# A state-space model and a feed-forward layer with looked-up weights: the order inside the layers' slots, and one gathered weight group fewer

## The chip, the cores and the metric

The kernel runs on one core of a Trainium2 chip. The core has five engines that run beside each other and meet in semaphores: TensorE (PE in the profile; its weight loads are PEld), VectorE (DVE), ScalarE (ACT), GpSimd (POOL) and SyncE (SP), which only starts transfers here. The metric is the time of one execution on the device, in microseconds (us): the median of three runs was 1264.0 us (1263.94 to 1266.96).

## The reference

The input x has 2048 tokens of 512 numbers. Two blocks follow each other, each added to its input and normalized over the 512 numbers:

```python
x = _layernorm(x + _L0_attn_ref(x, ...), axis=-1)
x = _layernorm(x + _L0_ffn_ref(x, codebook, idx_gate, idx_up, idx_down), axis=-1)
```

The first block projects to 64 numbers a token and runs four layers, then projects back to 512. A layer is

```python
y = silu(layernorm(h, l1w, l1b))
y = sconv(y, pr + 1j * pi, lr + 1j * li)      # a convolution along the tokens with p ** t, p complex
h = h + y * scl
y = layernorm(h, l2w, l2b)
y = silu(einsum('bld,fd->blf', y, w1) + b1_)  # 64 -> 256
h = h + einsum('blf,df->bld', y, w2) + b2_    # 256 -> 64
```

The second block has three weight matrices, which are not given but looked up: each index picks 8 numbers of a codebook of 8192 rows.

```python
Wg = codebook[idx_gate].reshape(1376, 512)    # also Wu, and Wd of 512 x 1376
h = silu(x @ Wg.T) * (x @ Wu.T)
return h @ Wd.T
```

## The kernel before, in words

**Weights.** The 1376 inner rows are cut into eleven tiles k of 128 (the last has 96, `REST`). Each tile has a gate unit 2k and an up unit 2k + 1. A unit has four turns of four quads; a quad is a quarter of a turn. PE looks a quad up: DVE compares the low index bits with constants and writes one-hots (`one_hots`, L1057), PE multiplies the codebook (in two parts) by them in eight matmuls (`candidates`), DVE keeps the candidate whose high bits fit (`choose`, L1075), and after the four quads of a turn PE adds up with four small matmuls against `adder` (`add_up`). The indices of a quad are spread over the partitions by a transfer of SP (`spread_parts`). At the end of a unit ACT copies the sum as the weight's high part (`keep_picked`, L459) and DVE makes the low part (`keep_rest`). For some units, listed in `POOLED`, the first turn isn't looked up: POOL gathers its 16 columns with 16 indirect transfers (`gather_up`, L389), and PE adds them with sixteen transposes (`turn_up`). `POOLED` holds the ten up units below 20 and the gate units of the tiles in `BOTH`. The down weights are all gathered by POOL (`gather_down`, L400, 16 x 4 for each full tile), and PE transposes them (`turn_down`, L924). `UP_AFTER` says after how many groups of 16 down gathers each `gather_up` stands in POOL's queue.

**The layers.** h is kept as 64 channels (twice, for the real and the imaginary part) by 2048 tokens, cut in `NC` = 4 chunks of 512. One slot t is one chunk c = t % 4 in one layer l = t // 4; there are 16. PE, DVE and ACT each have a written order for a slot, and the parts of several items lie in one slot: the first half of item t, the second norm and the 64-to-256 product of item t - 2, the way back of item t - 3. In each slot one or two quads of the look-up are placed as well (two in slots 0, 4, 8 and 12). The steps: `square1`, `variance1`, `root1`: the first norm; `xn`, Silu, `u`: its product and the turning back by `tab`; the scan (L1304) gives `g`; `d`, whose semaphore is `damped`, is g times `tab`; `turn` (L652, one column) carries the state to the next chunk, and DVE copies it (`state`, L1282). `mixed` is the matmul of d by `mix` into bank 0, `add_mixed` adds it to h. Then `square2`, `variance2` (into bank 2), `root2`, `norm2` (L1260), `spread` (two matmuls by w1t, into banks 1 and 2), `silus` (two Silus, which read these banks), `back` (two matmuls by w2t into bank 0) and `add_back` (L1267). Bank 2 thus serves `turn`, `variance2` and `spread`, and bank 0 serves `mixed` and `back`.

**Behind the layers** come the projection to 512, the norm, the transposes of x (`project`, `turn_x1`), then ten tiles k in each of which PE alternates a quad of a later tile's look-up with a share of tile k's gate and up products (`hidden`), and for each pair of tiles 16 products with the down weights (`down`). The last tile and its `down` end the kernel; their down weights are POOL's last gathers.

Matmuls recorded through the helper `mm` all have line L652, DVE's two-operand steps through `tt` line L1033.

Of the kernel before, what the change touches and what calls it, by code (L numbers as in the profile page):

```python
# [25 lines left out]
def build(nc, a, out):  # L26
# [6 lines left out]
    NC = T // C  # L33
# [15 lines left out]
    BOTH = (0, 5)  # L49
    POOLED = sorted([2 * k + 1 for k in range(FULL)] + [2 * k for k in BOTH])  # L50
    UP_AFTER = (0, 0, 4, 7, 13, 17, 20, 24, 25, 26, 30, 33)
# [16 lines left out]
    ITEMS = L * NC  # L68
# [91 lines left out]
    with ctx:  # L160
# [115 lines left out]
        s = {n: sem(n) for n in sem_names}  # L276
# [135 lines left out]
        def _(act):  # L412
# [130 lines left out]
            for t in range(ITEMS):  # L543
                root1(t)
                if t >= 2:
                    root2(t - 2)
                lay = cols[:, t // NC, :]
                act.wait_ge(s["normed1"], t + 1)
                if t:
                    act.wait_ge(s["scanned"], t)  # L550
                act.activation(y, xn, ACT.Silu, bias=lay[:, LN1_B:LN1_B + 1], scale=lay[:, LN1_W:LN1_W + 1]).then_inc(s["silu_made"], 1)
                if t:
                    square2(t - 1)
                if t >= 2:
                    silus(t - 2)
                square1(t + 1)

                act.preload_act_table(ACT.Abs_reciprocal_sqrt)
                while kept < unit_of(quads_in(t)[0]):
                    keep_picked(kept)  # L560
                    kept += 1


            root1(ITEMS)
# [85 lines left out]
        def _(pe):  # L650
# [197 lines left out]
            def mixed(i):  # L848
                pe.wait_ge(s["damped"], i + 1)
                if i >= 3:  # L850
                    pe.wait_ge(s["h_made"], i - 2)
                mm(bank[0][:, :], mix[:, i // NC, :], d).then_inc(s["mixed"], 1)
# [18 lines left out]
            def back(i):  # L871
                pe.wait_ge(s["ff_made"], i + 1)
                pe.wait_ge(s["h_mid"], min(ITEMS, i + 3))
                if i:
                    pe.wait_ge(s["h_made"], i)
                for k in range(FK):
                    done = mm(bank[0][:, :], w2t[:, i // NC, k, :], ff[:, k, :], k == 0, k == FK - 1)
                done.then_inc(s["ff_back"], 1)
# [10 lines left out]
            for t in range(ITEMS):  # L889
                quads = quads_in(t)  # L890
                if t % NC:

                    pe.wait_ge(s["scanned"], t)
                    if t >= 3:
                        pe.wait_ge(s["ff_made"], t - 2)
                    mm(bank[2][:, 0:1], turn[:, t // NC, :], g[:, C - 1:C]).then_inc(s["rotated"], 1)
                if t:
                    mixed(t - 1)
# [5 lines left out]
                candidates(quads[0])  # L904
                if t >= 2:
                    spread(t - 2)
                for quad in quads[1:]:
                    candidates(quad)
                for quad in quads:
                    add_up(quad - 1)  # L910
# [112 lines left out]
        def _(v):  # L1023
# [253 lines left out]
            for t in range(ITEMS):  # L1277
# [5 lines left out]
                if t:  # L1283
                    add_mixed(t - 1)
                one_hots(quads[0] + 1)
                v.wait_ge(s["rs1_made"], t + 1)
# [7 lines left out]
                if t >= 2:  # L1294
                    norm2(t - 2)
                if t >= 3:
                    add_back(t - 3)
                v.wait_ge(s["silu_made"], t + 1)
                tt(u, y, tab[:, l, :], ALU.mult).then_inc(s["turned_back"], 1)
                v.wait_ge(s["turned_back"], t + 1)  # L1300
                if c:
# [3 lines left out]
                                     ).then_inc(s["scanned"], 1)  # L1305
                v.wait_ge(s["scanned"], t + 1)
                if t:
                    v.wait_ge(s["mixed"], t)
                tt(d, g, tab[:, l, :], ALU.mult).then_inc(s["damped"], 1)
                choose(quads[0])  # L1310
                for quad in quads[1:]:
                    one_hots(quad + 1)
                    choose(quad)
# [125 lines left out]
```

## Time and profile before

| | us |
|---|---|
| median of three runs | 1264.0 |
| profiled execution | 1264.5 |
| its span, first to last instruction | 1262.5 |
| PE busy | 1188.8 (94%) |
| DVE busy | 1011.6 (80%) |
| POOL busy | 929.9 (74%) |
| ACT busy | 261.7 (21%) |
| mean granted clock of PE | 0.982 |

The busy time of an engine is the sum of its instructions, overlaps counted once. Idle time is put down to whoever released the engine. The page's chain follows the end of the program back; where two engines finish close to each other it names only the later one. The layers run from about 88 to 240 us, the tiles k = 0 to 9 from about 290 to 1200 us, and the rest is the last tile.

### The profile page before, as it was taken

To read this page: it belongs to the slowest core of one execution; us is meant where nothing else is said; L and a number is where in the kernel's file an instruction comes from. 1 tells how busy PE (TensorE), PEld (TensorE's weight loads), DVE (VectorE), ACT (ScalarE), POOL (GpSimd) and SP (SyncE) were. 2 spreads that over 40 slices of the span, in tenths; PEclk is the share of its full clock that TensorE was granted. 3 is DMA by queue.
4 is the path that set the end of the run, shared out by engine and by line. 5 is a ranking of instruction groups with operands and counts; after the bars stand their busy time and mean duration, and the time that the engine had idled before them with its cause. 6 is when DMAs were issued, how large, how long until landed. Compare 5 with 4: busy or idle time off the path is not lost.

```text
span 1262.5 us, 16835 instructions
## 1 busy us (share of the span) xinstructions
PE 1188.8 (94%) x5595; PEld 839.3 (66%) x5595; DVE 1011.6 (80%) x2194; ACT 261.7 (21%) x395; POOL 929.9 (74%) x895
## 2 busy tenths in 40 slices
PE   6857998889999999999999999999999999999998
PEld 4533444346777777777777777777777777778876
DVE  3998898878997778888777888778888778888845
ACT  2325777772000000000000000000000000000024
POOL 6777777777777777777777777777777777777710
PEclk8968999989999999999999999999999999999999
DMA  9331211102433223433223433333433333334303
GB/s 202 64 68 37 45 37 39 27 4 53 105 92 87 65 71 80 95 82 92 65 69 79 89 85 81 65 70 86 93 85 87 67 70 79 94 72 88 60 2 133
DMA packets 96971, 93.57 MB, mean 74 GB/s; under 512 B 53549, under 2 KB 57909, under 8 KB 96886
## 3 DMA queue, kind: packets, MB, share of 16 engines
q1 hardware_dynamic: 64692, 83.86, 23.0%
q0 software_dynamic: 28160, 3.66, 8.5%
q10 hardware_dynamic: 4034, 4.98, 1.4%
q8 instruction: 45, 0.74, 0.3%
q14 instruction: 40, 0.33, 0.1%
HBM read 87.53 MB, written 4.90 MB: 73 GB/s over the span
## 4 chain that ended last, share of the span: by engine, by line
POOL 73%; issue 21%; PE 4%; DMA 1%; DVE 0%; ACT 0%; POOLq 0%; SPq 0%; DVEq 0%
POOL stage_down L400 57%; POOL stage_up L389 16%; PE bank L652 2%; PE cand L652 2%; DMA work<-in_L_ffn_idx_up 0%; DMA stage_down<-in_L_ffn_codebook,idx_down 0%; ACT x L505 0%; POOLq L160 0%; DVE chosen L1229 0%; DVE x L1033 0%; PE bank L924 0%; SPq L315 0%; DVE idx_low L1091 0%; DVE idx_low L1092 0%; DVE shift L1239 0%
## 5 line engine op out<-in xcount | busy, mean ns | idle before, releaser
L400 POOL DMA_INDIRECT stage_down<-in_L_ffn_codebook,idx_down x688 | 722.3, 1050 | 209.7 <-issue 209.1
L652 PE MATMUL cand<-one_hot,book 128*128 128x512 f32 (+1 forms) x2432 | 622.7, 398 | 19.0 <-DVE one_hot L1057 19.0
L1057 DVE TENSOR_SCALAR one_hot<-bc,low_of 128x512 fp32r<-128x512 uint16 (+1 forms) x1216 | 512.8, 482 | 99.0 <-PE cand L652 97.3
L652 PEld LDWEIGHTS cand<-one_hot,book 128*128 128x128 f32 x2432 | 449.7, 189 | 187.2 <-DVE one_hot L1057 51.8
L389 POOL DMA_INDIRECT stage_up<-in_L_ffn_codebook,idx_up x192 | 205.6, 1071 | 63.8 <-issue 58.2
L652 PE MATMUL bank<-x1t_hi,w 128*128 128x512 f32 (+1 forms) x704 | 239.1, 396 | 0.0
L1075 DVE SCALAR_TENSOR_TENSOR chosen<-bc,high_of,cand 128x512 f32<-128x512 uint16 (+1 forms) x304 | 220.2, 724 | 21.1 <-PE bank L652 17.9
L652 PEld LDWEIGHTS bank<-x1t_hi,w 128*128 128x128 f32 (+1 forms) x704 | 130.3, 185 | 31.4 <-issue 2.1
L652 PE MATMUL bank<-x1t_lo,w 128*128 128x512 f32 (+1 forms) x352 | 137.7, 391 | 0.0
L598 ACT ACTIVATE prod<-bank 128x512 f32<-128x512 f32 (+1 forms) x44 | 26.3, 599 | 389.4 <-PE bank L652 389.4
L605 ACT ACTIVATE act_hi<-prod 128x512 fp32r<-128x512 f32 x40 | 25.3, 633 | 342.5 <-DVE prod L1033 342.5
L652 PE MATMUL bank<-wd,act_hi 128*128 128x512 f32 x272 | 84.5, 392 | 3.1 <-DVE x L1033 3.1
L652 PE MATMUL bank<-chosen,adder 128*32 128x512 f32 (+1 forms) x608 | 79.0, 591 | 0.0
L1033 DVE TENSOR_TENSOR x<-x,bank 128x512 f32<-128x512 f32 x76 | 51.7, 681 | 33.3 <-PE bank L652 33.3
L652 PEld LDWEIGHTS bank<-x1t_lo,w 128*128 128x128 f32 (+1 forms) x352 | 65.2, 185 | 15.8 <-issue 1.4
L652 PEld LDWEIGHTS bank<-wd,act_hi 128*128 128x128 f32 x272 | 50.8, 188 | 15.6 <-DVE x L1033 4.8
L652 PE MATMUL bank<-wd,act_lo 128*128 128x512 f32 x136 | 53.2, 391 | 0.0
L1033 DVE TENSOR_TENSOR prod<-prod,bank 128x512 f32<-128x512 f32 (+1 forms) x44 | 29.9, 679 | 22.1 <-PE bank L652 22.0
L459 ACT ACTIVATE w<-bank 128x512 fp32r<-128x512 f32 (+1 forms) x22 | 12.9, 588 | 118.4 <-PE bank L652 118.4
L652 PE MATMUL bank<-work,mean_p 64*128 64x512 f32 x72 | 28.1, 706 | 7.9 <-issue 7.1
L652 PE MATMUL bank<-work,w2t 128*128 128x512 f32 x64 | 34.4, 663 | 0.4 <-issue 0.4
L427 ACT ACTIVATE work<-bank,eps 128x512 f32<-128x512 f32 x36 | 23.2, 683 | 29.6 <-PE bank L652 29.5
(181 smaller groups left out, 751.8 us busy)
## 6 DMA issues: line engine op xcount, KB each, us to landing
bc<-index_parts SPq DMA_DIRECT2D x272, 256.0 KB, 3.3
stage_down<-in_L_ffn_codebook,idx_down POOLq DMA_INDIRECT x688, 2.7
bc<-index_parts_rest SPq DMA_DIRECT2D x32, 192.0 KB, 3.1
x<-in_L_attn_x ACTq DMA_DIRECT2D x4, 1024.0 KB, 9.8
out_x<-x SPq DMA_DIRECT2D x16, 256.0 KB, 2.0
stage_up<-in_L_ffn_codebook,idx_up POOLq DMA_INDIRECT x192
index_parts<-parts_t SPq DMA_DIRECT2D x20, 32.0 KB, 2.0
w_in<-in_L_attn_W ACTq DMA_DIRECT2D x2, 256.0 KB
```

The costliest lines, as they stand in the source:

```text
L389: pool.indirect_dma_start(stage_up[n % UPS][:, j * CS:(j + 1) * CS], None, a["L0_ffn_codebook"], bass.IndirectOffsetOnAxis(ap=idx_up[:, pl ...
L400: pool.indirect_dma_start(stage_down[k % RING][:, q, j * CS:(j + 1) * CS], None, a["L0_ffn_codebook"], bass.IndirectOffsetOnAxis(ap=idx_do ...
L427: return act.activation(dst, src, ACT.Abs_reciprocal_sqrt, bias=eps[0:dst.shape[0], :])
L459: act.activation(w[unit % WRING][:, 0, :, 0:nw], bank[3 + unit % 2][:, 0:KT * nw].rearrange("p (q n) -> p q n", q=KT), ACT.Copy).then_inc( ...
L598: act.activation(prod[0:n, c % 2, :], bank[0][0:n, :], ACT.Silu).then_inc(s["gate_silu"], 1)
L605: act.activation(act_of(k)[0][0:n, c * C:(c + 1) * C], prod[0:n, c % 2, :], ACT.Copy).then_inc(s["act_hi_made"], 1)
L652: return pe.matmul(dst, lhs, rhs, start=start, stop=stop)
L1033: return v.tensor_tensor(o, x0, x1, op)
L1057: done = v.tensor_scalar(one_hot[quad % 2][:, q, 0:nw], bc[quad % BCS][:, 0:nw], low_of[:, q:q + 1], None, ALU.is_equal)
L1075: v.scalar_tensor_tensor(chosen[quad % CHOSEN][:, 0:nw], bc[quad % BCS][:, nw:2 * nw], high_of[:, 0:1], cand[cand_of(quad)][:, 0:nw], ALU. ...
```

## The change

In the layers, the order inside a slot changes on three engines.

- PE: the slot's first quad goes to its head, ahead of `turn`; `mixed` of the item before goes from behind `turn` to behind `spread`; the adder of a turn that the quad before has ended goes ahead of `spread`. `mixed` now waits for `h_mid` of the item before and for one more `h_made`; `back` waits for one `h_mid` fewer.
- DVE: `add_mixed` goes from the head of the slot to behind the scan; `norm2` goes ahead of `xn`; all one-hots of the slot go to its head, and `choose` ahead of `u`.
- ACT: `square2` of an item stands at the head of the next slot, not behind the Silu of the same.

Beside it, `BOTH` loses tile 5: the first turn of gate unit 10 isn't gathered any more but looked up, so POOL has eleven gathered groups and PE 308 quads in place of 304. `UP_AFTER` puts the last three gathers at 27, 31 and 34 groups.

```diff
-    BOTH = (0, 5)
+    BOTH = (0,)
-    UP_AFTER = (0, 0, 4, 7, 13, 17, 20, 24, 25, 26, 30, 33)
+    UP_AFTER = (0, 0, 4, 7, 13, 17, 20, 24, 27, 31, 34)
@@ ACT
             for t in range(ITEMS):
+                if t >= 2:
+                    square2(t - 2)
                 root1(t)
...
-                if t:
-                    square2(t - 1)
...
+            square2(ITEMS - 2)
             root1(ITEMS)
@@ PE
             def mixed(i):
                 pe.wait_ge(s["damped"], i + 1)
-                if i >= 3:
-                    pe.wait_ge(s["h_made"], i - 2)
+                if i:
+                    pe.wait_ge(s["h_mid"], i)
+                if i >= 2:
+                    pe.wait_ge(s["h_made"], min(ITEMS - NC + 1, i - 1))
...
-                pe.wait_ge(s["h_mid"], min(ITEMS, i + 3))
+                pe.wait_ge(s["h_mid"], i + 2 if i < ITEMS - 3 else ITEMS)
...
                 quads = quads_in(t)
+                candidates(quads[0])
                 if t % NC:
...
-                if t:
-                    mixed(t - 1)
                 variance1(t)
                 if t >= 2:
                     variance2(t - 2)
                 if t >= 3:
                     back(t - 3)
-                candidates(quads[0])
+                add_up(quads[0] - 1)
+                for quad in quads[1:]:
+                    candidates(quad)
                 if t >= 2:
                     spread(t - 2)
+                if t:
+                    mixed(t - 1)
                 for quad in quads[1:]:
-                    candidates(quad)
-                for quad in quads:
                     add_up(quad - 1)
@@ DVE
-                if t:
-                    add_mixed(t - 1)
                 one_hots(quads[0] + 1)
+                if t >= 2:
+                    norm2(t - 2)
+                for quad in quads[1:]:
+                    one_hots(quad + 1)
...
-                if t >= 2:
-                    norm2(t - 2)
                 if t >= 3:
                     add_back(t - 3)
+                for quad in quads:
+                    choose(quad)
...
+                if t:
+                    add_mixed(t - 1)
                 v.wait_ge(s["scanned"], t + 1)
-                if t:
-                    v.wait_ge(s["mixed"], t)
                 tt(d, g, tab[:, l, :], ALU.mult).then_inc(s["damped"], 1)
-                choose(quads[0])
-                for quad in quads[1:]:
-                    one_hots(quad + 1)
-                    choose(quad)
```

PE in one slot of the layers with one quad, before (`mean_p` are the two variances, `w2t` is back, `w1t` is spread):

```order
L652 MATMUL bank<-work,turn 128x1
L652 MATMUL bank<-work,mix 128x512
L652 MATMUL bank<-work,mean_p 128x512 x2
L652 MATMUL bank<-work,w2t 128x512 x2
L652 MATMUL cand<-one_hot,book 128x512 x8
L652 MATMUL bank<-work,w1t 128x512 x2
L652 MATMUL bank<-chosen,adder 32x512 x4
```

PE in the slot of the same place, changed:

```order
L653 MATMUL cand<-one_hot,book 128x512 x8
L653 MATMUL bank<-work,turn 128x1
L653 MATMUL bank<-work,mean_p 128x512 x2
L653 MATMUL bank<-work,w2t 128x512 x2
L653 MATMUL bank<-chosen,adder 32x512 x4
L653 MATMUL bank<-work,w1t 128x512 x2
L653 MATMUL bank<-work,mix 128x512
```

The quad has gone ahead of `turn`, the mix behind the spread, and the adder ahead of the spread.

DVE in such a slot, before (from the top: state copy, the add of the mix, one-hots, `xn`, norm2, add_back, `u`, the scan, `d`, choose):

```order
L1282 COPY state<-bank 128x1
L1033 TENSOR_TENSOR h<-h,bank 128x512
L1057 TENSOR_SCALAR one_hot<-bc,low_of 128x512 x4
L1033 TENSOR_TENSOR work<-h,work 128x512
L1260 SCALAR_TENSOR_TENSOR work<-h,cols,work 128x512
L1267 SCALAR_TENSOR_TENSOR h<-bank,cols,h 128x512
L1033 TENSOR_TENSOR work<-work,tab 128x512
L1304 SCALAR_TENSOR_TENSOR work<-cols,state,work 128x512
L1033 TENSOR_TENSOR work<-work,tab 128x512
L1075 SCALAR_TENSOR_TENSOR chosen<-bc,high_of,cand 128x512
```

DVE, changed:

```order
L1286 COPY state<-bank 128x1
L1061 TENSOR_SCALAR one_hot<-bc,low_of 128x512 x4
L1264 SCALAR_TENSOR_TENSOR work<-h,cols,work 128x512
L1037 TENSOR_TENSOR work<-h,work 128x512
L1271 SCALAR_TENSOR_TENSOR h<-bank,cols,h 128x512
L1079 SCALAR_TENSOR_TENSOR chosen<-bc,high_of,cand 128x512
L1037 TENSOR_TENSOR work<-work,tab 128x512
L1310 SCALAR_TENSOR_TENSOR work<-cols,state,work 128x512
L1037 TENSOR_TENSOR h<-h,bank 128x512
L1037 TENSOR_TENSOR work<-work,tab 128x512
```

The add of the mix has gone from the second place to the last but one, norm2 ahead of `xn`, and choose ahead of `u`.

POOL's queue around the gathers of units 9 to 15, the difference (- before, + changed; a `stage_up` row of 16 is one unit):

```order
 L389 DMA stage_up<-in_L_ffn_codebook,idx_up 128x8 x16
-L400 DMA stage_down<-in_L_ffn_codebook,idx_down 128x8 x16
-L389 DMA stage_up<-in_L_ffn_codebook,idx_up 128x8 x16
-L400 DMA stage_down<-in_L_ffn_codebook,idx_down 128x8 x16
+L400 DMA stage_down<-in_L_ffn_codebook,idx_down 128x8 x48
 L389 DMA stage_up<-in_L_ffn_codebook,idx_up 128x8 x16
```

One unit's 16 gathers are gone, and those behind it stand with more down gathers between them.

## Rows read from the trace of the kernel before

**Rows 1.** The page: part 1, part 4 by engine, a line of part 5.
```profile
PE 1188.8 (94%) x5595; PEld 839.3 (66%) x5595; DVE 1011.6 (80%) x2194; ACT 261.7 (21%) x395; POOL 929.9 (74%) x895
...
POOL 73%; issue 21%; PE 4%; DMA 1%; DVE 0%; ACT 0%; POOLq 0%; SPq 0%; DVEq 0%
...
L389 POOL DMA_INDIRECT stage_up<-in_L_ffn_codebook,idx_up x192 | 205.6, 1071 | 63.8 <-issue 58.2
```
**Rows 2.** Timeline, 1203 to 1207: start, length, engine, line, [idle before, releaser].
```profile
1203.63 0.94 POOL L400 DMA_INDIRECT stage_down<-in_L_ffn_codebook,idx_down  x1 [0.30 <-issue]
...
1206.07 0.61 PE L924 MATMUL bank<-ident,stage_down 128*96 128x128 f32 x4 [0.34 <-DMA stage_down<-in_L_ffn_codebook,idx_down]
```
**Rows 3.** Waits of PE: us in total, times, longest.
```profile
PE bank L924 <- DMA stage_down<-in_L_ffn_codebook,idx_down: 0.3, 1, 0.3
```
**Rows 4.** Timeline of PE in slot 10 of the layers.
```profile
182.14 0.35 PE L652 MATMUL bank<-work,turn 128*128 128x1 f32 x2 [0.46 <-ACT work L539]
...
184.45 1.98 PE L652 MATMUL bank<-work,w2t 128*128 128x512 f32 x4
...
188.23 1.13 PE L652 MATMUL bank<-work,w1t 64*128 64x512 f32 x4
190.81 0.35 PE L652 MATMUL bank<-work,turn 128*128 128x1 f32 x2 [1.46 <-ACT work L539]
```
**Rows 5.** Timeline of DVE in slot 10.
```profile
183.50 0.69 DVE L1033 TENSOR_TENSOR h<-h,bank 128x512 f32<-128x512 f32 x1 [0.81 <-PE bank L652]
184.10 1.67 DVE L1057 TENSOR_SCALAR one_hot<-bc,low_of 128x512 fp32r<-128x512 uint16 x4
...
187.98 0.69 DVE L1033 TENSOR_TENSOR work<-work,tab 128x512 f32<-128x512 f32 x1 [0.28 <-ACT work L551]
...
190.65 0.74 DVE L1075 SCALAR_TENSOR_TENSOR chosen<-bc,high_of,cand 128x512 f32<-128x512 uint16 x1
191.31 0.15 DVE L1282 COPY state<-bank 128x1 f32<-128x1 f32 x1
```
**Rows 6.** Timeline of ACT in slot 10.
```profile
189.40 1.26 ACT L539 ACTIVATE work<-bank,cols 128x512 f32<-128x512 f32 x2 [0.94 <-PE bank L652]
```
**Rows 7.** Timeline of DVE: `d` of slots 3 and 15, the memsets behind the loop.
```profile
124.50 0.69 DVE L1033 TENSOR_TENSOR work<-work,tab 128x512 f32<-128x512 f32 x1
...
235.67 0.69 DVE L1033 TENSOR_TENSOR work<-work,tab 128x512 f32<-128x512 f32 x1
...
237.18 1.03 DVE L1318 MEMSET work<- 1x512 f32 x2 [0.16 <-issue]
```
**Rows 8.** Timeline in slot 9: state copy, second variance, its root.
```profile
174.52 0.14 DVE L1282 COPY state<-bank 128x1 f32<-128x1 f32 x1
...
174.77 1.09 PE L652 MATMUL bank<-work,mean_p 64*128 64x512 f32 x2 [0.32 <-issue]
...
175.90 0.69 ACT L427 ACTIVATE work<-bank,eps 128x512 f32<-128x512 f32 x1 [0.73 <-PE bank L652]
```
**Rows 9.** Timeline of PE: an adder round in slot 6.
```profile
153.09 1.06 PE L652 MATMUL bank<-chosen,adder 128*32 128x512 f32 x8
```
**Rows 10.** Timeline of ACT: the copy of gate unit 0.
```profile
127.82 0.60 ACT L459 ACTIVATE w<-bank 128x512 fp32r<-128x512 f32 x1
```
**Rows 11.** Timeline of PE: transposes of the down weights, k = 3, 5, 7.
```profile
575.47 0.60 PE L924 MATMUL bank<-ident,stage_down 128*128 128x128 f32 x4
...
759.65 0.60 PE L924 MATMUL bank<-ident,stage_down 128*128 128x128 f32 x4
...
951.73 0.60 PE L924 MATMUL bank<-ident,stage_down 128*128 128x128 f32 x4
```
**Rows 12.** Windows: stretch, busy of PE, PEld, DVE, ACT, POOL, PE's clock, DMA.
```profile
104.00:108.00 4.00, 2.91 (x6) 1.32 (x8) 2.52 (x5) 1.20 (x1) 3.08 (x4) 0.50 0.15 36
```
**Rows 13.** Timeline of PE in slot 2.
```profile
104.95 0.59 PE L652 MATMUL bank<-work,turn 128*128 128x1 f32 x2 [4.08 <-DVE work L1304]
```

## The prediction

> **What bounds the kernel now.** I began with the busy times and then read the end of the trace. TensorE (PE) is busy 94% of the span, VectorE (DVE) 80%, GpSimd (POOL) 74% [rows 1]. The page's chain of waits gives 73% to POOL, so I looked where its stream of gathers meets PE. The last gather starts at 1203.63; PE, out of other work, stands idle 0.34 us until it has landed and transposes it at 1206.07 [rows 2]. The list of PE's waits has no other one for a gather [rows 3]. So the two long streams, PE's matmuls and POOL's gathers, end within 0.34 us of each other, and the chain names POOL because it came last by that little. A gather costs POOL (205.6 + 63.8) / 192 = 1.40 us with the gap ahead of it [rows 1]. A change that frees POOL alone gives back 0.3 us; the rest is PE's own sum.
>
> PE has holes in the layers. A slot there is one chunk of 512 tokens through one layer. Slot 10 goes from the `turn` matmul at 182.14 to the next at 190.81, 8.67 us, 1.46 us of it idle [rows 4]. The order is turn, mix, variances, back, quad, spread; then `turn` waits for ScalarE (ACT), which reads bank 2 in the two Silus from 189.40 [rows 6]. DVE loses time in the same slot: 0.81 us before it adds the mix at 183.50, and 0.28 us before 187.98, for ACT's Silu [rows 5]. From 183.50 to the state copy at 191.31 are 7.81 us, so its work there is 7.53 us. From `damped` of slot 3 (124.50) to that of slot 15 (235.67), twelve slots, pass 111.2 us [rows 7].
>
> **The reordered slots.** Nothing is added; each instruction keeps its duration. Three moves count: PE puts the quad ahead of `turn` and the mix last, so that ACT's Silus run beside a quad; DVE adds the mix after the scan, when it is long there; ACT squares the sum at the head of the next slot.
>
> PE's hole goes. What is late next is DVE's norm2. With the state copy as 0, the second variance may start at 0.25 (174.52 to 174.77) and its root at 1.38 (175.90); the root takes 0.69, so norm2 starts at 2.11 [rows 8]. The one-hots (1.6 us, from 184.10 [rows 5]) are done by 1.7: DVE stands 0.4 us. The rest of its slot is 7.53 - 1.59 = 5.94 us, less some 0.1 where instructions that don't depend on each other now stand side by side: the next copy comes at 7.96. PE's own work in a slot is 8.67 - 1.46 = 7.2 us [rows 4]; that it must wait for the copy between `turn` and the variance makes it 7.6, hidden. With an adder (1.0 us [rows 9]) it needs 8.6, and then it is PE that ends last; before, an adder lay in PE's hole and cost nothing.
>
> Slots 4 to 15: three have two quads, 7.96 + 1.6 for the one-hots and 0.66 for choose (190.65 to 191.31 [rows 5]), the copy left out, 10.15 each, 30.5 in all; seven plain ones of 8.0, 56.0; two with an adder, 17.2. The sixteen transposes of gate unit 1 add 0.9. In slot 3 those of unit 0 and its adder now stand ahead of spread, 1.9 us, and ACT then copies the gate weight (0.60 [rows 10]) ahead of the square for which the variance and norm2 wait: slot 4 takes 2.5 us more. The copy in slot 13 costs 1.1 in slot 14. The sum is 108.2 against 111.2: 3.0 us gained. Bounds: DVE without a wait would need 9 x 7.6 + 3 x 9.8 = 97.8 us, 13.4 gained; with 8.67 in every plain slot, as today, and the costs of slots 4 and 14 on top, 2 us are lost. I take the worked sum: each piece of it stands in a row, and neither bound has a row for its dependencies.
>
> Behind the loop, two memsets of `hn` (1.03 us from 237.18 [rows 7]) lie between `choose` and the last add of the mix. `choose` is gone from there, and the memsets fall beside the last mix matmul: 0.7 us gained. In slot 0 a quad at the low clock now precedes the first variance and both chooses precede the scan, some 4 us later in all; slots 1 to 3 lose the holes of up to 4.08 us that PE has there. I count 0.5 gained, between 3 lost and 4 gained. The layers in all: 3.0 + 0.7 + 0.5 = 4.2 us.
>
> **The sixth gate unit looked up.** POOL loses 16 gathers, 16 x 1.40 = 22 us. PE gets four quads of eight matmuls and one adder round more and sixteen transposes fewer, DVE four sets of one-hots and chooses, SP four loads of indices (beside all else, as they are now). All of it falls between the transposes of the down weights of k = 3 and k = 5. The trace has the price: 575.47 to 759.65, with 52 quads, are 184.18 us; 759.65 to 951.73, with 56 and else the same jobs, 192.08 us [rows 11]. The difference, 7.9 us, is read net, with DVE's part and the transposes in it, and is not hidden: it lies on PE's stream. Bounds: at PE's own pace a quad is 3.78 - 1.98 = 1.8 us [rows 4], so 7.2 + 1.0 - 0.9 = 7.3; were DVE the limit, 4 x (1.59 + 0.66) = 9.0.
>
> POOL then ends 22 us earlier, so its slack behind PE becomes about 25 us, and PE's wait of 0.34 us goes.
>
> The matmul share of 94% and the weight loads' (PEld) 66% [rows 1] differ much. The Trainium skill ("Perfetto Trace Analysis", Identifying the Most-Contended Engine) holds the matmul share for a poor measure of headroom and the weight loads' share for the good one. By that rule a third of PE is free, the look-up would hide, and the sum would be 7.9 lower. The trace does not agree: four quads more cost 7.9 us between the transposes.
>
> **The sum.** 1264.5 (the profiled execution, 2.0 above its span) + 7.9 - 4.2 - 0.3 = 1267.9. That execution is 0.5 above the median of 1264.0, so 1267.4.
>
> **Rivals,** from the median.
> A, the slots close up. Without the wait for norm2 and the long slots 4 and 14, DVE is the bound, at 97.8 us: 13.4 + 0.7 + 0.5 gained, 1264.0 + 7.9 - 14.6 - 0.3 = 1257.0; half way there is 1262. For it: DVE's work is only 7.53 us a slot. Against: norm2 waits for a chain of copy, variance and root that can't begin before the copy.
> B, slower, by the clock. From 104 to 108 us PE was granted 0.50, its level of 1.2 GHz, [rows 12], after 4.08 us idle before the `turn` at 104.95 [rows 13]. In the new order PE's idle time is in pieces (before `turn`, before the variance, before spread), in slots 1 to 4 together 1.5 to 3 us a slot. Where a slot falls to 1.2 GHz, PE's 7.6 us become 11 or more and it is PE that ends the slot, 2 to 3 us later. Two such slots more than today take the 4.2 us: 1264.0 + 7.9 - 0.3 = 1271.6. It beats the forecast from about 2 us of such loss.
> C, the look-up is hidden: PE's four quads go into gaps that the matmul share doesn't show, and only the layers count: 1264.0 - 4.2 - 0.3 = 1259.5. For it, PEld's 66%; against it, rows 11.
> D, no change: the layers gain about 8 us, half way to A, and the look-up takes it: 1264.
>
> **How the numbers follow.** Measurements of this kernel tell nothing below about 0.3%, 3.8 us: faster is under 1260.2, slower over 1267.8. Forecast (1264 to 1271) 0.54, of it 0.26 slower and 0.28 within; A 0.14, of it 0.12 faster; B 0.12, slower; C 0.04, faster; D 0.16, of it 0.02 faster. Together faster 0.18, within 0.3% 0.44, slower 0.38. The time is the forecast's. The range goes half way toward A's price and over B's, 1259.5 to 1272.
>
> **What would show it.** The transposes of k = 3 and k = 5 are 192.1 us apart. The last gather starts about 1182, and the last transposes wait for no DMA. A plain slot is 8.0 us from copy to copy, with 0.4 us before norm2, for ACT; `turn` waits for ACT's Silus no more; a slot with an adder is near 8.7; slot 4 is the longest. From `damped` 3 to `damped` 15 are 108 us: under 103, A; PE at 0.50 in more slots than today, B; a stretch from k = 3 to k = 5 that grows by under 5 us, C. The forecast is wrong if the layers gain less than 1 or more than 8 us.

## The result, and the profile after

The changed kernel takes 1280.4 us (median; 1279.4 to 1283.0), the kernel before 1265.5 in the same comparison: ratio 1.0111, 95% interval 1.0091 to 1.0131. It is slower by 14.9 us. The forecast was 1267.4, with a range of 1259.5 to 1272.0, so it was wrong, by 13 us. The profiled execution took 1279.4 us, with a span of 1277.6 (before 1264.5 and 1262.5).

The page of the kernel after, busy times, chain by engine and the gathers of the up weights, against [rows 1]:

```profile
PE 1216.6 (95%) x5603; PEld 851.8 (67%) x5603; DVE 1022.1 (80%) x2213; ACT 264.6 (21%) x395; POOL 913.8 (72%) x879
...
PE 86%; DVE 8%; ACT 2%; issue 2%; DMA 1%; SPq 1%; DVEq 0%; ACTq 0%
...
L389 POOL DMA_INDIRECT stage_up<-in_L_ffn_codebook,idx_up x176 | 186.6, 1060 | 58.5 <-issue 53.4
```

PE was busy 1188.8 us and is now busy 1216.6. The chain has gone over from POOL to PE, as it should when the gathers end early. Timeline of the kernel after, POOL's last gather, and PE's transposes of the down weights of k = 3, 5 and 7, against [rows 2, 11]:

```profile
1182.08 1.05 POOL L400 DMA_INDIRECT stage_down<-in_L_ffn_codebook,idx_down  x1 [0.30 <-issue]
```
```profile
579.31 0.60 PE L928 MATMUL bank<-ident,stage_down 128*128 128x128 f32 x4
...
772.67 0.60 PE L928 MATMUL bank<-ident,stage_down 128*128 128x128 f32 x4
...
966.05 0.60 PE L928 MATMUL bank<-ident,stage_down 128*128 128x128 f32 x4
```

From k = 3 to k = 5 pass 193.4 us instead of 184.2. But from k = 5 to k = 7, where the two programs issue the same jobs, pass 193.4 us as well, where it was 192.1. PE is slower at work that the change doesn't touch. The groups of PE in the window from 300 to 1200 us say which (busy, mean ns of one), first before, then after:

```profile
L652 PE MATMUL cand<-one_hot,book 128*128 128x512 f32 x1928 | 495.7, 399 | 4.5 <-DVE one_hot L1057 4.5
L652 PE MATMUL bank<-x1t_hi,w 128*128 128x512 f32 x621 | 208.3, 391 | 0.0
L652 PE MATMUL bank<-wd,act_hi 128*128 128x512 f32 x256 | 79.5, 392 | 3.1 <-DVE x L1033 3.1
```
```profile
L653 PE MATMUL cand<-one_hot,book 128*128 128x512 f32 x1968 | 507.0, 399 | 4.5 <-DVE one_hot L1061 4.4
L653 PE MATMUL bank<-x1t_hi,w 128*128 128x512 f32 x607 | 206.3, 395 | 0.0
L653 PE MATMUL bank<-wd,act_hi 128*128 128x512 f32 x256 | 80.4, 395 | 3.1 <-DVE x L1037 3.1
```

The matmuls over `x1t` and `wd` take 395 ns instead of 391 or 392. Those over `one_hot` show no difference in whole nanoseconds; the mean over their instructions in the two traces, to one place more, is 398.6 before and 399.2 after. There are some 1460 of the first kind in the program and 2208 of the second.

The layers. DVE of the kernel after, in slots 3 and 4, then 10 to 11 and 15, against [rows 5, 7]; below it PE at the head of slot 11, against [rows 4]:

```profile
127.03 0.69 DVE L1037 TENSOR_TENSOR work<-work,tab 128x512 f32<-128x512 f32 x1
...
131.53 0.75 DVE L1264 SCALAR_TENSOR_TENSOR work<-h,cols,work 128x512 f32<-128x512 f32 x1 [2.23 <-ACT work L427]
...
189.20 1.28 DVE L1310 TENSOR_TENSOR_SCAN work<-cols,state,work 128x512 f32<-128x512 f32 x1
...
193.82 0.75 DVE L1264 SCALAR_TENSOR_TENSOR work<-h,cols,work 128x512 f32<-128x512 f32 x1 [0.51 <-ACT work L427]
...
197.12 1.28 DVE L1310 TENSOR_TENSOR_SCAN work<-cols,state,work 128x512 f32<-128x512 f32 x1
...
235.00 0.69 DVE L1037 TENSOR_TENSOR work<-work,tab 128x512 f32<-128x512 f32 x1
```
```profile
188.60 2.42 PE L653 MATMUL cand<-one_hot,book 128*128 128x512 f32 x8
190.86 0.28 PE L653 MATMUL bank<-work,turn 128*128 128x1 f32 x2
191.07 1.99 PE L653 MATMUL bank<-work,mean_p 64*128 64x512 f32 x4
```

`turn` waits for nothing. A plain slot takes 7.92 us (189.20 to 197.12), 0.51 of it before norm2, and slot 4 has the long wait before norm2, 2.23 us. From `damped` of slot 3 to that of slot 15 are 235.00 - 127.03 = 107.97 us, against 111.17. But `damped` of slot 3 comes 2.53 us later than before. One part of that PE shows in slot 0: the candidates wait for DVE's one-hots, and the variance, which was first before, stands behind them:

```profile
88.82 3.75 PE L653 MATMUL cand<-one_hot,book 128*128 128x512 f32 x8 [8.00 <-DVE one_hot L1061]
92.50 2.07 PE L653 MATMUL bank<-work,mean_p 64*128 64x512 f32 x2
```

Last, PE's clock in the projection behind the layers. Windows (stretch; busy of PE, PEld, DVE, ACT, POOL; granted clock), before, then after:

```profile
252.00:260.00 8.00, 5.06 (x9) 2.19 (x10) 3.03 (x8) 6.52 (x11) 6.12 (x7) 0.64 0.07 3
...
268.00:276.00 8.00, 6.49 (x26) 3.24 (x26) 7.61 (x19) 5.94 (x11) 6.05 (x7) 1.00 0.08 5
```
```profile
252.00:260.00 8.00, 6.18 (x11) 2.45 (x12) 2.79 (x7) 5.39 (x10) 6.00 (x7) 0.66 0.08 5
...
268.00:276.00 8.00, 8.00 (x21) 4.21 (x19) 6.88 (x17) 4.93 (x10) 5.87 (x8) 0.52 0.08 3
```

Both executions have the fall at 252 us. The one of the kernel after has a second: 0.52 means that nearly all of the stretch was at PE's lower level, 1.2 GHz, and PE does 21 matmuls instead of 26 in the same 8 us.

Added up between points that both traces have: to `damped` 3 +2.5; from there to `damped` 15 -3.2; on to the first transposes of down weights (304.79 before, 307.14 after) +3.0; on to those of k = 9 (1180.37 and 1195.93) +13.2; to the end -0.5. Together +15.1, the difference of the spans.

### The profile page after: what moved, and what is told of

It reads as the page before. It is cut to its first block, busy times and chain, and to the rows that moved or that the text cites. A ratio compares the mean times of both kernels' runs of the same rounds, so it can differ in the third digit from the quotient of the medians.

```text
span 1277.6 us, 16858 instructions
## 1 busy us (share of the span) xinstructions
PE 1216.6 (95%) x5603; PEld 851.8 (67%) x5603; DVE 1022.1 (80%) x2213; ACT 264.6 (21%) x395; POOL 913.8 (72%) x879
## 4 chain that ended last, share of the span: by engine, by line
PE 86%; DVE 8%; ACT 2%; issue 2%; DMA 1%; SPq 1%; DVEq 0%; ACTq 0%
PE cand L653 44%; PE bank L653 40%; DVE one_hot L1061 2%; DVE work L1037 1%; DMA book_in<-in_L_ffn_codebook 1%; PE cand L833 1%; DVE chosen L1079 1%; DVE small L1037 1%; DVE work L1310 1%; SPq L321 1%; DVE x L1037 0%; PE bank L928 0%; ACT work L427 0%; ACT x L505 0%; DMA bc<-index_parts 0%
## 5 line engine op out<-in xcount | busy, mean ns | idle before, releaser
L653 PE MATMUL cand<-one_hot,book 128*128 128x512 f32 (+1 forms) x2464 | 633.4, 399 | 25.4 <-DVE one_hot L1061 25.3
L1061 DVE TENSOR_SCALAR one_hot<-bc,low_of 128x512 fp32r<-128x512 uint16 (+1 forms) x1232 | 521.7, 485 | 101.8 <-PE cand L653 100.5
L653 PEld LDWEIGHTS cand<-one_hot,book 128*128 128x128 f32 x2464 | 456.2, 189 | 195.2 <-issue 54.9
L653 PE MATMUL bank<-x1t_hi,w 128*128 128x512 f32 (+1 forms) x704 | 242.8, 400 | 0.0
L1079 DVE SCALAR_TENSOR_TENSOR chosen<-bc,high_of,cand 128x512 f32<-128x512 uint16 (+1 forms) x308 | 223.2, 725 | 23.0 <-PE bank L653 17.2
L389 POOL DMA_INDIRECT stage_up<-in_L_ffn_codebook,idx_up x176 | 186.6, 1060 | 58.5 <-issue 53.4
L653 PE MATMUL bank<-work,mean_p 64*128 64x512 f32 x72 | 36.5, 664 | 1.2 <-ACT work L470 0.8
L653 PEld LDWEIGHTS bank<-chosen,adder 128*32 128x32 f32 x616 | 13.0, 108 | 26.1 <-issue 23.9
## 6 DMA issues: line engine op xcount, KB each, us to landing
bc<-index_parts_rest SPq DMA_DIRECT2D x32, 192.0 KB, 3.0
```

The costliest lines, as they stand in the source:

```text
L389: pool.indirect_dma_start(stage_up[n % UPS][:, j * CS:(j + 1) * CS], None, a["L0_ffn_codebook"], bass.IndirectOffsetOnAxis(ap=idx_up[:, pl ...
L653: return pe.matmul(dst, lhs, rhs, start=start, stop=stop)
L1061: done = v.tensor_scalar(one_hot[quad % 2][:, q, 0:nw], bc[quad % BCS][:, 0:nw], low_of[:, q:q + 1], None, ALU.is_equal)
L1079: v.scalar_tensor_tensor(chosen[quad % CHOSEN][:, 0:nw], bc[quad % BCS][:, nw:2 * nw], high_of[:, 0:1], cand[cand_of(quad)][:, 0:nw], ALU. ...
```

## The experiments

The runs are named by their labels. Eight of them (e1 to e6, u1, u2) fell on three chips on which the kernel before takes 2167 to 2201 us. That is told at the end; from them only durations of single matmuls are used. The ten others ran on two chips, g0 to g3 and h1 to h4 on one, t1 and t2 on the other; on the first the kernel before takes 1266.7 us, on the second 1266.1 (46 executions in all).

**The parts one by one, and the kernel again (e3, e5, e6, e4).** e5 is the kernel after with the twelve groups of before; e6 is the kernel before with the eleven of after:

```diff
 e5, against after            e6, against before
-BOTH = (0,)                 -BOTH = (0, 5)
+BOTH = (0, 5)               +BOTH = (0,)
 (UP_AFTER with its twelve,   and with its eleven entries)
```

> The same kernel as in e1: the new slots, twelve gathered groups. If the slower pace comes with the slots: 1271 to 1273 us (ratio 1.005) and 193.4 us from tile 1 to tile 3; if it comes with the look-up or with the execution: 1266 to 1268, and 192.1 us. If the gathers of GpSimd set the end: 1264.5 to 1266 and a wait of the last turn_down for its gather. The second fall of the clock near 270 us is there in every case.

> The same kernel as in e2: the slots of before, the sixth gate unit looked up. The runs of e1 to e4 fell on a chip on which the kernel before takes 2201 us instead of 1264, because the broadcasts of the indices land late, so they can't tell the terms of a sum over TensorE's work. Expectations as they stood: sum of the recorded steps 1271.5 to 1272 us (ratio 1.006); if the slower pace of 0.67% comes with the look-up, 1277 to 1278 (1.010) and 193.4 us from the turn_down of tile 1 to that of tile 3; no second fall of the clock at 270 us if that fall belongs to the slots.

> The changed kernel once more, as a control on the chip of the other three. If the 0.67% slower pace of the main stage belongs to the program, tile 1 to tile 3 takes 193.4 us here, beside 192.1 for the kernel before; if it is of the execution or of the chip, the distance is 192.1 here, or varies, and the time falls to some 1274 to 1276. The second fall of the clock near 270 us: there again if it follows from the program's idle times, and worth 2.9 us.

Measured: ratios 0.991 (e5, 95% interval 0.987 to 0.995), 1.000 (e6) and 0.995 (e3, 0.991 to 0.998) to a kernel before that takes 2168 to 2201 us there. e1 and e2, the same kernels as e5 and e6 on another such chip, gave 0.994 and 1.000. These say nothing of a sum over PE's work. The matmuls do. PE's groups from 940 to 980 us, where PE had next to no wait, of e5, then of e6:

```profile
L653 PE MATMUL bank<-x1t_hi,w 128*128 128x512 f32 x31 | 10.5, 391 | 0.0
```
```profile
L652 PE MATMUL bank<-x1t_hi,w 128*128 128x512 f32 x31 | 10.6, 395 | 0.0
```

e3 shows 394. Over 560 to 2100 us, where the means of `x1t` are mixed with stretches at the lower clock, those of `wd` say the same: 392 (e5), 394 (e6), 395 (e3). So the pace goes with the look-up, not with the slots, and it is of the program, not of an execution or a chip.

What the look-up also does: `idx_up` is allocated with `len(POOLED)` places of 16 numbers, 768 bytes a partition with twelve and 704 with eleven. All tiles allocated behind it move down by 64 bytes: those of the layers (`work`, `h`, `tab` and others), and `x1t`, `act`, `wd`, `prod`. Added up over the allocations, `x1t` starts 64 bytes past a multiple of 128 before and on a multiple of 128 after; the trace doesn't show addresses.

> The changed kernel, but slot 0 in the order of before: TensorE takes variance1(0) ahead of the candidates that wait for one_hots(8), and VectorE does the extra one_hots and choose of slot 0 behind d. Theory (the layers start late because their first matmul stands behind candidates that wait for VectorE): scan 0 falls from 100.5 to some 94 to 96 us, scan 3 from 124.8 to 122 to 123, and the time by 2 to 3 us, to 1277.5. Rival (the layers are bound in slots 1 to 3 by TensorE's half clock and its idle, so the start is caught up with): scan 3 stays at 124 to 125 and the time within 0.5 us of the changed kernel's.

e4, the kernel after with slot 0 in the order of before, is inconclusive: it ran on such a chip too (ratio 0.990), and scan 0 came at 213 us there. h3 below takes up its question.

**Four kernels without the gathers (g0 to g3).** In all four the looked-up rows are left out: each staging tile is filled by one plain DMA of other rows of the codebook, so the weights made from it are wrong ones, while PE, DVE and ACT issue the same instructions:

```diff
-for j in range(JD):
-    pool.indirect_dma_start(stage_up[n % UPS][:, j * CS:(j + 1) * CS], None, codebook, ...)
+pool.dma_start(stage_up[n % UPS][:, :], some_rows)
 (the same for stage_down; the waits' numbers follow)
 g2 besides:
 idx_up = sb("idx_up", [P, len(POOLED), JD], I32)
+spare = sb("spare", [P, 16], I32)
```

> The kernel before with its 880 row gathers left out: each staging tile of up and down weights comes by one plain DMA of 128 rows of the codebook (so the values that follow from it are other ones, while every other instruction stays). It is the base for the three runs below. On the chip of e1 to e6 the kernel before takes 2170 to 2200 us because the index broadcasts do not land while a run of gathers is being issued. If that is the mechanism, this kernel is bound by TensorE there too and takes 1255 to 1270 us, with 192.1 us from the turn_down of tile 1 to that of tile 3. If the broadcasts are slow for another reason: above 1500 us.

> The new slots with twelve gathered groups, gathers left out as in g0. Against g0: slots 4 to 15 -2.8, slots 0 to 3 and the layers' start +2, the second fall of the clock near 270 us +2.9, the drain -0.5: together +1 to +2.5 us. If the clock's second fall was a matter of one execution: -1.5 to 0. The pace of the main stage is that of g0 (192.1 us from tile 1 to tile 3), for e5, with the new slots alone, shows 391 ns for a matmul over x1t as the kernel before does.

> The changed kernel, gathers left out as in g0, with 64 bytes a partition put behind idx_up. Theory L: dropping one group from idx_up moved x1t, act and wd down by 64 bytes a partition, and a matmul that streams them takes 394 to 395 ns instead of 391. With the 64 bytes given back the matmuls over x1t and wd take 391 to 392 ns, tile 1 to tile 3 takes 192.1 us, and the time is that of g3 plus the look-up alone, 7.9 us. Rival: the pace follows the number of gathered groups or the round that is added, then 395 ns and 193.4 us stay, and the time is g3 plus 13.

> The changed kernel, gathers left out as in g0, nothing else. By theory L: 395 ns for the matmuls over x1t and wd, 193.4 us from tile 1 to tile 3, and 5 to 6 us more than g2; against g0 +14 to +15.5, as the changed kernel stands to the kernel before. Rival (the slower pace needs the gathers beside it): as g2, 391 ns.

| run | slots | groups, pad | median us | k = 3 to k = 5 | x1t, ns |
|---|---|---|---|---|---|
| g0 | before | 12 | 1268.3 | 184.2 | 391 |
| g3 | new | 12 | 1266.2 | 184.2 | 391 |
| g2 | new | 11, 64 bytes | 1273.9 | 192.0 | 391 |
| g1 | new | 11 | 1279.6 | 193.3 | 395 |

Theory L holds: 64 bytes of nothing are worth 5.6 us (g1 against g2). The look-up alone is 7.7 us (g2 against g3). That the slots gain 2.1 us (g3 against g0) is less than the spread of g0 (1263.5 to 1269.8), and the two profiled executions stand the other way (1267.7 and 1265.3), so these two runs don't decide it. The 14 to 15.5 us that g1 was to stand above g0 came out as 11.3, or 12.9 above the kernel before with its gathers; that part of its expectation is missed. g0 was to tell also what makes the other chips slow; it fell on a chip that isn't slow, so it doesn't. It tells something else, in its windows:

```profile
252.00:260.00 8.00, 7.15 (x11) 3.06 (x12) 3.08 (x8) 4.42 (x8) 0.00 (x0) 0.50 0.01 2
...
268.00:276.00 8.00, 8.00 (x20) 4.14 (x18) 6.86 (x16) 5.29 (x10) 0.00 (x0) 0.50 0.00 0
```

The second fall of the clock is there with the slots of before; h4 below has it with them and with the gathers (0.58), and h3, with the new slots, hasn't (1.00). So it is not of the new slots.

**With the gathers, and the layout theory tried (h1, h2, h4).**

```diff
 h1, against after: spare (64 bytes a partition) allocated behind idx_up
 h2, against after: spare (64 bytes a partition) allocated ahead of one_hot
 h4, against before: as e6
```

> The changed kernel with its gathers, and 64 bytes a partition behind idx_up. If g2 carries over: matmuls over x1t and wd 391 to 392 ns instead of 394 to 395, 192.1 us from tile 1 to tile 3, and 1273.5 to 1275.5 us, 5 to 6 below the changed kernel, 7 to 9 above the kernel before. Rival (with the gathers beside it something else sets the pace): 1278 to 1281. A chip that starves the index broadcasts would show the matmuls' durations all the same.

> The changed kernel with the 64 bytes a partition put ahead of one_hot instead of behind idx_up: one_hot, chosen, bc, w and x1t all move up by 64 bytes, so that x1t, act and wd stand where they stand in the kernel before (64 past a multiple of 128), and one_hot, chosen and w, which stood there, stand on a multiple of 128. If the pace of a matmul follows the address of what it streams: over x1t and wd 391 to 392 ns, over one_hot 402 to 403 instead of 399, and the time is 3 to 9 us above h1, since the 2464 matmuls over one_hot pay what the 1500 others regain. If it follows the distance between the streamed and the loaded tile: x1t stays at 395 (w moves with it), and one_hot changes because book does not move. If one_hot is not sensitive at all: as h1.

> The slots of before with the sixth gate unit looked up and its places dropped (eleven groups), as e2 and e6, for a time on an undisturbed chip. By the terms measured so far (extra round 7.9, 64 bytes 5.7): 13 to 14 us above the kernel before, ratio 1.0103 to 1.0112, 193.3 us from tile 1 to tile 3. Rival (the layout costs only with the new slots): ratio 1.006.

h1: 1273.8 us, ratio 1.0054 (1.0037 to 1.0070). Its groups and its transposes of k = 3 and 5, 191.9 us apart:

```profile
L654 PE MATMUL bank<-x1t_hi,w 128*128 128x512 f32 x603 | 202.9, 391 | 0.0
...
L654 PE MATMUL bank<-wd,act_hi 128*128 128x512 f32 x256 | 79.5, 392 | 3.1 <-DVE x L1038 3.1
```
```profile
577.87 0.60 PE L929 MATMUL bank<-ident,stage_down 128*128 128x128 f32 x4
...
769.81 0.60 PE L929 MATMUL bank<-ident,stage_down 128*128 128x128 f32 x4
```

The lost 5.5 to 6.6 us are the layout's, with the gathers too. They are not in the layers, whose tiles move as well: the sixteen scans of h1 start within 0.04 us of those of the kernel after. h4: 1280.0 us, ratio 1.0104 (1.0089 to 1.0119): look-up and layout cost with the old slots what they cost with the new.

h2: 1282.1 us, ratio 1.0125 (1.0109 to 1.0140), and its groups:

```profile
L654 PE MATMUL cand<-one_hot,book 128*128 128x512 f32 x1968 | 507.5, 400 | 4.7 <-DVE one_hot L1062 4.7
L654 PE MATMUL bank<-x1t_hi,w 128*128 128x512 f32 x598 | 203.1, 394 | 0.0
...
L654 PE MATMUL bank<-wd,act_hi 128*128 128x512 f32 x256 | 80.3, 395 | 3.1 <-DVE x L1038 3.1
```

`x1t`, `act` and `wd` stand at the same bytes as in h1 and are slow all the same; `one_hot`, for which 402 to 403 ns was the first expectation, takes 400 (399.6, against 398.7 in h1). So the address of what is streamed does not set the pace by itself. Nor does the distance within one matmul: `wd` and `act` keep theirs in every kernel here.

**Where in the layout (t1, t2, u1, u2).** All are the kernel after with spare bytes: t1 64 ahead of `one_hot`, 64 ahead of `w`, 64 behind `idx_up`; t2 32 ahead of `book`, 96 ahead of `one_hot`, 64 behind `idx_up`; u1 128 and u2 32 behind `idx_up`.

> The changed kernel with 64 bytes a partition put in at three places: ahead of one_hot, ahead of w and behind idx_up. one_hot, chosen and bc stand on a multiple of 128 bytes; w, x1t, act and wd stand 64 past one, as in the kernel before. h2 left two theories. M (the loaded and the streamed tile of one matmul must stand alike, or w's own place counts): matmuls over x1t 391 ns. N (what counts is how the tiles that TensorE streams stand to those that VectorE and the DMAs use beside it, one_hot, chosen and bc): 394 to 395 ns for x1t and for wd. That wd and act stand in h2 where they stand in h1, and take 393 to 395 ns against 391 to 392, speaks for N. Time: 1273 to 1275 us by M, 1279 to 1283 by N.

> The changed kernel with 32 bytes a partition ahead of book, 96 ahead of one_hot and 64 behind idx_up: book and adder now stand 64 bytes past a multiple of 128 too (they stand 32 past one in all kernels so far), and one_hot, chosen, bc, w, x1t, act and wd as in the kernel before. If the place of book against one_hot costs the 2464 matmuls over one_hot what 64 bytes cost those over x1t: 395 ns or less instead of 399, 8 to 10 us, so 1264 to 1266 us, ratio 0.998 to 1.000. If a tile's 32 bytes don't matter: as h1, 1273.8 us, 399 ns.

> The changed kernel with 128 bytes a partition behind idx_up, so that x1t, act and wd stand on a multiple of 128 again, 64 past where the kernel before has them. If the place counts modulo 128 bytes: 394 to 395 ns for x1t and wd, 193.3 us from tile 1 to tile 3, 1279 to 1282 us. If only the shortened idx_up was bad and any place from before's on is good: 391 to 392 ns and 1273 to 1275 us.

> The changed kernel with 32 bytes a partition behind idx_up: x1t, act and wd stand 32 bytes past a multiple of 128, half-way. If the pace falls off with the distance from before's place: 392 to 394 ns, 1275 to 1278 us (t1 and t2, at 393 and 392 ns, show that there are values between). If 64-byte places are special: at least 395 ns and 1280 us or more.

PE's `x1t` group of t1, t2 (300 to 1190 us) and u1 (940 to 980):

```profile
L656 PE MATMUL bank<-x1t_hi,w 128*128 128x512 f32 x601 | 203.4, 393 | 0.0
```
```profile
L656 PE MATMUL bank<-x1t_hi,w 128*128 128x512 f32 x601 | 202.8, 392 | 0.0
```
```profile
L654 PE MATMUL bank<-x1t_hi,w 128*128 128x512 f32 x30 | 10.1, 396 | 0.0
```

Start byte modulo 128, and mean ns:

| kernels | one_hot | w | x1t, act, wd | x1t_hi | wd, act_hi |
|---|---|---|---|---|---|
| before, e5, g0, g3, h1, g2, h3 | 64 | 64 | 64 | 391 to 392 | 392 |
| t2 (`book` at 64, else at 32) | 64 | 64 | 64 | 392 | 392 |
| t1 | 0 | 64 | 64 | 393 | 393 |
| h2 | 0 | 0 | 64 | 394 | 395 |
| u2 | 64 | 64 | 32 | 394 to 395 | 393 to 396 |
| after, e3, e6, g1, h4 | 64 | 64 | 0 | 394 to 395 | 395 |
| u1 | 64 | 64 | 0 | 394 to 396 | 391 to 395 |

The best place is the one the kernel before has by chance. No kernel came below 391 in these groups, and the matmuls over `one_hot` stay between 398.6 and 399.6 whatever moves, so t2's hope is refuted (1275.0 us, ratio 1.0071). t1 took 1277.1 (1.0088). Neither M nor N holds: t1 lies between them. u1 is as slow as the kernel after, so 128 bytes are no change of place, as its first expectation had it; u2, half-way, is as slow too, and not between. The total times of u1 and u2 say nothing of either, for they ran on the slow chips. That the layout sets the pace is shown, by spare bytes alone; by what path is open.

**The slots alone, slot 0 mended (h3).** The kernel after with twelve groups, and in slot 0 the order of before:

```diff
 on PE
-candidates(quads[0])
+if t:
+    candidates(quads[0])
 ...
     back(t - 3)
+if not t:
+    candidates(quads[0])
 on DVE: in slot 0 choose, and the one_hots of the second quad, behind d
```

> The new slots with twelve gathered groups, and slot 0 in the order of before on TensorE and VectorE (variance1(0) ahead of the candidates that wait for one_hots(8); the extra one_hots and choose behind d). Theory: scan 0 at 94 to 95 us (100.5 in the changed kernel, 94.0 before), scan 3 at 121.5 to 123, and the layers end 2.5 to 3.5 us earlier than before; but the gathers of GpSimd end where they did (1203.6 us), so the last turn_down waits for them some 2 to 3 us and the time is that of the kernel before, ratio 0.998 to 1.001. Rival (the layers' gain is real at the end too): ratio 0.996 to 0.998. If slots 1 to 3 absorb the early start: scan 3 at 124.8 and ratio 1.000 to 1.002.

1265.8 us, ratio 0.9991 (0.9981 to 1.0001). Scans of slots 0 and 3, kernel before, after, h3:

```profile
93.98 1.28 DVE L1304 TENSOR_TENSOR_SCAN work<-cols,work 128x512 f32<-128x512 f32 x1
...
123.18 1.28 DVE L1304 TENSOR_TENSOR_SCAN work<-cols,state,work 128x512 f32<-128x512 f32 x1
```
```profile
100.47 1.28 DVE L1310 TENSOR_TENSOR_SCAN work<-cols,work 128x512 f32<-128x512 f32 x1
...
124.81 1.29 DVE L1310 TENSOR_TENSOR_SCAN work<-cols,state,work 128x512 f32<-128x512 f32 x1
```
```profile
93.59 1.28 DVE L1313 TENSOR_TENSOR_SCAN work<-cols,work 128x512 f32<-128x512 f32 x1
...
125.60 1.28 DVE L1313 TENSOR_TENSOR_SCAN work<-cols,state,work 128x512 f32<-128x512 f32 x1
```

Slot 0 is mended, 6.9 us earlier than in the kernel after, and nothing of it is left at slot 3, as its third expectation had it (the ratio is that of the first). The candidates moved out of slot 0's way now wait at its end (first row below, PE), and PE is at 0.50 in the window from 112 to 116 us. At the other end POOL's gathers come too late for PE, twice:

```profile
97.95 3.16 PE L653 MATMUL cand<-one_hot,book 128*128 128x512 f32 x8 [2.21 <-DVE one_hot L1064]
...
952.41 0.63 PE L931 MATMUL bank<-ident,stage_down 128*128 128x128 f32 x4 [1.97 <-DMA stage_down<-in_L_ffn_codebook,idx_down]
...
1207.53 0.61 PE L931 MATMUL bank<-ident,stage_down 128*96 128x128 f32 x4 [0.96 <-DMA stage_down<-in_L_ffn_codebook,idx_down]
```

The first transposes of down weights start 1.6 us earlier than before (303.23 us against 304.79), and these two waits of 1.97 and 0.96 us take it back. So with twelve groups POOL takes the layers' gain; with eleven the look-up costs more than the layers give. On these two chips no version is measurably faster than the kernel before.

## Why the prediction was wrong

- **The step that failed** is the term of the look-up, "PE gets four quads of eight matmuls and one adder round more and sixteen transposes fewer", +7.9 in all, and with it the premise of the sum, "each instruction keeps its duration". The 7.9 itself is right: from k = 0 to k = 9 h1 takes 883.3 us and the kernel before 875.6, 7.7 more. But the same edit shortens `idx_up`, and the tiles behind it move; that costs 5.5 us in the same stretch (888.8 against 883.3), 5.6 and 6.6 by the medians of g1 against g2 and of the kernel after against h1 (these two not measured side by side). Of the 5.5 us some 4 are on `x1t` and `wd` (about 1300 matmuls in that stretch, 3 to 3.4 ns each) and some 1 on `one_hot` (about 2000, half a nanosecond each), an estimate from the means of the two traces. The sum had no such term, and no rival either. The source shows it: `idx_up` is allocated with `len(POOLED)` places, and the diff shortens `POOLED`.
- **Slots 4 to 15** were worked out at -3.0 and gave -3.2. Plain slots (8.0, measured 7.92), the wait before norm2 (0.4, 0.51), slots with two quads (10.15, 10.17) and slot 4 as the longest came as said; a slot with an adder takes 8.92, not 8.6. Rival A, the slots closing up, is out: norm2 does wait for the chain of variance and root.
- **Slots 0 to 3** were put at -0.5, between 3 lost and 4 gained; `damped` 3 is 2.5 us late. The 4 us of slot 0 were named, and 6.5 by scan 0; that slots 1 to 3 would give them back and more was wrong: they gave back 4.9 of the 6.5 by scan 3 (1.6 late), and `d`, which now stands behind the add of the mix, starts 2.22 us behind scan 3 instead of 1.32, the other 0.9. In h3, with slot 0 mended, scan 3 is no earlier, so slots 1 to 3 lose in it what slot 0 no longer does. By what is open. PE waits less for DVE's scan there than before (0.90 and 1.89 us against 4.08 and 1.90) and anew for norm2 ahead of spread (1.57); its granted clock from 88 to 132 us is 0.82 before, 0.81 after and 0.80 in h3, worth 1 us at most (an estimate: 0.02 of 44 us). It also takes more than one trace to size it: leaving out the slow chips, scan 3 comes between 122.8 and 126.6 us in the nine traces with the new slots, and between 120.9 and 123.2 in the three with the old.
- **The drain**: -0.7 was worked out; the loss of 3.0 us from `damped` 15 to the first transposes is net of it. The rest is the second fall of the clock, +3.5 or so, since scan 15 to those transposes takes 70.4 us without it (before) and 74.0 with it and the old slots (h4). With the second fall in both, h4 takes 72.7 us from `damped` 15 and the kernel after 72.1, so the -0.7 shows as -0.5. Rival B had a clock fall in mind, but in slots 1 to 4 and caused by the new order. g0 and h4 have this one with the old order, and h3 is without it with the new. Of the 46 executions of the kernel before on the two chips 29 have a mean clock of 0.978 or less, where all traces with the second fall lie (0.975 to 0.978), and their medians are 1266.1 and 1266.7; the profiled one (0.982, 1264.5) is of the fewer without, and only 2 of the 46 were as quick. So some 2 us of the forecast's error lie in its base, one execution and a median of three times, two of which were at the quick end; these 2 us are part of the 3.5, not on top of them. That this fall came here and not in the base is luck, and what sets it off is open.
- **The end**: the last gather was forecast for 1182 and starts at 1182.08; the wait of 0.34 is gone, as said.
- **The skill's rule.** Four quads more cost 7.7 us, look-up alone (g2 against g3), so rival C is out. By the Trainium skill ("Perfetto Trace Analysis", Identifying the Most-Contended Engine), which judges TensorE's headroom by the share of peak arithmetic and by the weight loads' busy share, the 66% of the second would have left room for them; the first was not worked out here. The trace, with PE's matmuls busy all but without a gap in that stretch, had none.

Taken together: forecast +3.4 on the profiled execution, layout +5.5, slots 0 to 3 +3.0, the clock's second fall +3.5 are 15.4; measured 14.9. The layout is the largest term of the error and the only one whose cause is shown by a change of that alone; without it the time, 1273.8 us in h1, is still outside the range.

## What to carry to other kernels

Count what a change of a list's length does to every tile sized by it: a tile that grows or shrinks moves all that are allocated behind it, and here 64 bytes cost seven tenths of what the intended work cost. When two programs issue the same jobs over a stretch and one is slower, compare the mean duration per group before looking for a wait; a difference of 3 to 4 ns in 391 was most of 5.5 us. And take the base of a sum from many executions: one profile is one draw of the clock's falls.

## What the runs showed that I had not expected

PE's pace at unchanged work depends on where the tiles lie, and on tiles that the matmul does not read: `wd` and `act` stand alike in h1 and h2 and take 392 and 395 ns.

Three chips run this kernel in 2167 to 2201 us instead of 1266, whichever version. Windows of e6, one in which POOL issues gathers without a pause, one without gathers:

```profile
1060.00:1080.00 20.00, 2.35 (x4) 0.94 (x4) 0.00 (x0) 0.00 (x0) 15.12 (x17) 0.50 0.07 3
...
1120.00:1140.00 20.00, 20.00 (x91) 15.23 (x90) 14.68 (x31) 1.83 (x3) 0.00 (x0) 1.00 0.21 66
```

While gathers are issued, the DMA engines are 7% busy and move 3 GB/s, and the broadcasts of the indices, on which DVE and through it PE wait, seem hardly to land (e6 puts 504.7 us of the waits of DVE's one-hots down to a transfer or another source outside the engines, shown as `remote`); when POOL pauses, PE is busy without a gap. That this is all of it is not shown: in e6 ACT's `prod` waits 487.7 us for `remote` too, and PE stands some 490 us between matmuls that wait for nothing the profile shows. On the two other chips gathers and broadcasts go on side by side. Why the chips differ is open: the kernels without gathers ran on a chip that doesn't show it. On the three chips the ranking is another one too: the slots alone gave ratios of 0.991 and 0.994, and u1 and u2, with the look-up, 0.989 and 0.992 (0.983 to 0.995 and 0.988 to 0.995).
